# Splitting queries and keys on POOL, and a new order of fills, in a 16-head attention kernel

## The chip, the cores and the metric

The kernel runs on one core of a Trainium2 chip. The metric is the device time of one execution in microseconds, the median of several runs. The engines are called PE (TensorE, matmuls), DVE (VectorE), ACT (ScalarE), POOL (GpSimd) and SP (the queue that issues most transfers).

## The reference, cut to what matters

`x` is 32 batches of 128 rows of width 128, with a condition vector and a context of 128 rows for each batch. The first block, all in float32:

```python
x_norm = modulate(_ln(x), shift_a, scale_a)             # self attention, 16 heads of 8
q, k, v = split(x_norm @ W_qkv + b_qkv)
attn = softmax(q @ k.T * 8 ** -0.5) @ v
x = x + gate_a[:, None] * (attn @ W_proj + b_proj)
q_c = _ln(x) @ W_qc + b_qc                              # cross attention
k_c, v_c = split(_ln(context) @ W_kvc + b_kvc)
x = x + softmax(q_c @ k_c.T * 8 ** -0.5) @ v_c @ W_cproj + b_cproj
x = x + gate_m[:, None] * (gelu(modulate(_ln(x), shift_m, scale_m) @ W_mlp1 + b_mlp1) @ W_mlp2 + b_mlp2)
```

A second block attends to 128 learned keys and mixes three small experts by a router. The change touches nothing of it.

## The kernel before, in words

**Tiling.** The batches form 8 groups of 4. Self and cross attention of every group make 16 half loads, of which each iteration i = 0 to 7 of `attention_loop` holds two ("memories" 0 and 1, table `HOLDS`). An iteration treats 8 batches ("cores" in the code), each in 4 units of 4 heads, so it has 32 steps of one unit; there are 256 units in all. For each unit PE computes the scores (L1683), DVE takes their negated row maxima over the keys (L1518, into `NM`), later PE computes the scores a second time, transposed and with the maxima subtracted (the "shifted" scores, L1696), ACT takes the exponential (L1399) and PE multiplies with the values (L1712). Scores run `LEAD` = 14 steps ahead of the shifted ones. Iteration -1 is the lead-in: only loads, norms, fills and the first 14 score units. Iterations 5 and 6 are called crossed: both memories hold cross attention and the steps come from `crossed_steps`; iterations 1 to 4 use `regular_steps`, 0 and 7 own mixtures.

**How the maxima enter.** Two batches make a pair, four pairs an iteration. After the last reduction of a pair, DVE splits the maxima into two bf16 parts `M2`: `high` (L1529, a copy that casts) and `low` (L1531, the difference). PE turns them (`max_turn`, L1724), ACT copies them (L1413), and SP moves them as extra rows into the query stack. `max_parts` and `max_turn` stand at steps 2, 10, 18 and 26.

**Queries and keys in three parts.** For an f32-like product of bf16 operands, q and k are split into high, middle and low bf16 parts (`Qp`, `Kp`). PE fills a bank with `W x XT` (the "fill", L1763), ACT reads it and writes the high part as bf16 with the bias added (L1454), DVE computes `rest = bank + bias - high` in f32 (L1630), and POOL makes the middle part, `rest` + 0 cast to bf16 (L1352), and the low part, `rest` - middle (L1355). SP then moves each part to 8-row strides of the stacks `Qs` and `Ks`, 6 moves for each of q and k (L1280); the first K of all goes by ACT's queue. Three stacks are used in turn. Stack 0 of the next iteration is first read by the score of step 18, stack 1 by that of step 34 (2 of the next iteration). All fills but a few of the first ones share one bank, PS6, so each waits until the one before has been read.

**Order.** No planner: every engine walks the same list of events, `attention_events`, sorted by the written times (in steps) of `regular_steps`, `crossed_steps`, `first_steps` and `stack_steps`, and does its own part of each event in that order. A `fill_steps(t, name, n, (part, at))` is PE's fill at t and the reads at `at` (part 0 is ACT's, part 1 DVE's and POOL's for q and k). `stats_steps` are layer norm statistics on DVE (L1571, L1579), with the reciprocal deviation on POOL (L1321, L1324); `norm_steps` are two POOL operations (L1342, L1345). `load_steps` is SP's load of a context group, which waits until the norm of the one before is done. Names such as k0, q1, v1 are the memory's; xt_s, xt_x, xt_c are the turned norms of self, cross query and context; proj and yt the projection and its turn back.

Of the kernel before, what the change touches and what calls it, by code (L numbers as in the profile page):

```python
# [21 lines left out]
ALU = mybir.AluOpType  # L22
# [3 lines left out]
P = 128  # L26
# [123 lines left out]
def regular_steps(i):  # L150
# [9 lines left out]
            + fill_steps(12.0, "proj_c", i - 3, (1, 12.1))  # L160
            + fill_steps(14.0, "yt_c", i - 3, (1, 14.1))
            + fill_steps(16.0, "xt_c", i - 1, (1, 16.1))
# [3 lines left out]
            + fill_steps(26.0, "v0", i + 1, (1, 26.1))  # L166
            + fill_steps(28.0, "proj_s", i + 2, (0, 28.1), (1, 28.2))
            + fill_steps(30.0, "yt_s", i + 2, (1, 30.1)))


def crossed_steps(i):

    g = 2 * i - 6
    return (load_steps(0.1, g + 1) + stats_steps(4.2, 5.2, "ln_c", g + 1) + norm_steps(6.0, "ln_c", g + 1)
            + stats_steps(11.2, 12.2, "ln_x", g + 1) + norm_steps(14.0, "ln_x", g + 1)
            + load_steps(9.0, g + 2) + stats_steps(18.2, 19.2, "ln_c", g + 2) + norm_steps(20.0, "ln_c", g + 2)
            + fill_steps(1.0, "xt_c", g, (1, 1.1)) + fill_steps(3.0, "k0", i + 1, (0, 3.1), (1, 4.0))
            + fill_steps(6.0, "xt_x", g, (1, 6.1)) + fill_steps(8.0, "q0", i + 1, (0, 8.1), (1, 9.0))
            + fill_steps(11.0, "v1", i, (1, 11.1))
            + fill_steps(13.0, "proj_c", i - 3, (1, 13.1)) + fill_steps(15.0, "yt_c", i - 3, (1, 15.1))  # L180
            + fill_steps(17.0, "xt_c", g + 1, (1, 17.1)) + fill_steps(19.0, "k1", i + 1, (0, 19.1), (1, 20.0))
            + fill_steps(22.0, "xt_x", g + 1, (1, 22.1)) + fill_steps(24.0, "q1", i + 1, (0, 24.1), (1, 25.0))
            + fill_steps(27.0, "v0", i + 1, (1, 27.1)))


# [1679 lines left out]
```

## Time and profile before

| | us |
|---|---|
| median of 3 runs | 617.23 (615.05 to 619.32) |
| profiled execution | 618.34, span 616.6 |
| PE busy | 558.4 (91%) |
| DVE busy | 445.8 (72%) |
| ACT busy | 379.8 (62%) |
| POOL busy | 221.0 (36%) |
| mean granted clock of PE | 0.962 |

Busy time is the time in which an engine runs at least one instruction; PE's matmuls overlap, so a busy PE need not be at its peak. The granted clock is a share of TensorE's full speed, 2.4 GHz; 0.5 is its lower level, 1.2 GHz. An idle engine costs nothing by itself; only the chain of waits tells what sets the end.

### The profile page before, as it was taken

The numbers are of one execution on the slowest core, as the hardware profiler recorded it, in microseconds if no ns is written. First come the engines' busy times: TensorE is split into PE (matmuls) and PEld (weight loads), VectorE is DVE, ScalarE is ACT, GpSimd is POOL, SyncE is SP. The second block draws the span as 40 slices with busy tenths as digits, with TensorE's granted clock in tenths as the row PEclk, the third lists the DMA queues.
The fourth block names the chain that finished last, engine by engine and source line by source line (L and its number), as shares of the span: only waits on it lengthen the run. The fifth ranks groups of instructions, "written<-read, shape, count | busy, mean of one in ns | idle before, by whom it ended". The sixth has DMA issues, their size and how long they took to land.

```text
span 616.6 us, 16374 instructions
## 1 busy us (share of the span) xinstructions
PE 558.4 (91%) x6153; PEld 388.7 (63%) x6153; DVE 445.8 (72%) x1233; ACT 379.8 (62%) x889; POOL 221.0 (36%) x246
## 2 busy tenths in 40 slices
PE   3668999999999988898899989988999999999995
PEld 2354566666666655565567634445788788788785
DVE  7587999999999887978775635554475775775555
ACT  2236778787787875766776654563554754754762
POOL 6735635364654346435501310223123123123100
PEclk9768999999999997988999999998999999999999
DMA  7523645344343234233300010000000001000000
GB/s 206 128 81 94 177 142 147 84 125 108 98 117 94 75 107 122 71 83 85 106 3 5 2 35 0 1 0 18 16 10 28 26 11 34 23 11 19 17 18 18
DMA packets 48554, 39.24 MB, mean 64 GB/s; under 512 B 6209, under 2 KB 47842, under 8 KB 48482
## 3 DMA queue, kind: packets, MB, share of 16 engines
q1 hardware_dynamic: 46296, 34.49, 20.7%
q10 hardware_dynamic: 2186, 3.77, 2.1%
q8 instruction: 47, 0.77, 0.5%
q14 instruction: 25, 0.20, 0.1%
HBM read 9.93 MB, written 2.10 MB: 20 GB/s over the span
## 4 chain that ended last, share of the span: by engine, by line
PE 60%; DVE 22%; ACT 8%; issue 6%; DMA 2%; ACTq 1%; SPq 0%; POOL 0%; DVEq 0%; POOLq 0%
PE PS L910 30%; DVE NM L1518 7%; PE PS L1712 6%; PE PS L1683 5%; PE PS L1763 4%; PE PS L1775 3%; PE PS L947 3%; DVE rest L1630 2%; PE PS L1768 2%; PE PS L1734 2%; DVE M L1529 2%; PE PS L1696 1%; PE PS L1756 1%; PE PS L1779 1%; DVE M L1531 1%
## 5 line engine op out<-in xcount | busy, mean ns | idle before, releaser
L1518 DVE TENSOR_REDUCE NM<-PS 128x4 f32<-128x512 f32 x256 | 163.1, 682 | 20.1 <-PE PS L1683 19.8
L1399 ACT ACTIVATE PR<-PS 128x512 f32<-128x512 f32 x256 | 139.8, 600 | 31.8 <-PE PS L1696 31.7
L1683 PE MATMUL PS<-Ks,Qs 64*128 64x128 bf16 x1024 | 85.2, 224 | 6.3 <-DVE NM L1518 3.9
L713 ACT ACTIVATE r_HID<-PS,ANC 128x128 f32<-128x128 f32 x224 | 63.2, 370 | 43.8 <-PE PS L910 43.7
L1683 PEld LDWEIGHTS PS<-Ks,Qs 64*128 64x128 bf16 x1024 | 59.6, 97 | 47.6 <-issue 25.2
L1696 PE MATMUL PS<-Qs,Ks 64*128 64x128 bf16 x1024 | 85.9, 222 | 2.1 <-ACT PR L1399 1.4
L1712 PE MATMUL PS<-PR,Va 128*32 128x128 f32 x2048 | 84.3, 283 | 0.0
L1712 PEld LDWEIGHTS PS<-PR,Va 128*32 128x32 f32 x2048 | 49.6, 111 | 29.5 <-ACT PR L1399 18.5
L1696 PEld LDWEIGHTS PS<-Qs,Ks 64*128 64x128 bf16 x1024 | 58.2, 95 | 6.9 <-ACT PR L1399 4.8
L910 PE MATMUL PS<-r_NXS,r_WNS 128*128 128x512 f32 x168 | 54.2, 431 | 5.2 <-ACT r_HID L713 5.2
L631 POOL TENSOR_TENSOR m_veps<-m_mv,m_eps 128x4 f32<-128x4 f32 x16 | 3.2, 201 | 143.5 <-DVE m_mv L787 143.5
L910 PE MATMUL PS<-r_EVS,r_US 128*128 128x512 f32 x168 | 47.7, 392 | 0.0
L910 PE MATMUL PS<-WO,r_HID 128*128 128x128 f32 x384 | 45.5, 275 | 0.0
L910 PEld LDWEIGHTS PS<-WO,r_HID 128*128 128x128 f32 x384 | 44.7, 192 | 0.7 <-ACT r_HID L713 0.2
L1763 PE MATMUL PS<-XT,W 128*128 128x512 f32 x64 | 39.9, 712 | 4.4 <-ACT XT L1435 4.4
L910 PEld LDWEIGHTS PS<-r_NXS,r_WNS 128*128 128x128 f32 x168 | 28.6, 189 | 14.5 <-ACT r_HID L713 8.0
L910 PEld LDWEIGHTS PS<-r_EVS,r_US 128*128 128x128 f32 x168 | 31.5, 188 | 7.4
L910 PE MATMUL PS<-m_H,W 128*128 128x512 f32 x64 | 33.7, 628 | 1.5 <-DVE YT L810 1.5
L1352 POOL TENSOR_TENSOR Kp<-rest,zeros 128x512 bf16<-128x512 f32 x16 | 16.6, 1038 | 48.4 <-DVE rest L1630 48.4
L693 ACT ACTIVATE m_H<-PS,V 128x512 f32<-128x512 f32 x32 | 21.3, 693 | 19.7 <-PE PS L910 19.7
L910 PE MATMUL PS<-m_XT,W 128*128 128x512 f32 x64 | 32.1, 601 | 0.3 <-ACT m_XT L705 0.3
L1321 POOL TENSOR_TENSOR veps<-mv,eps 128x4 f32<-128x4 f32 x24 | 4.8, 202 | 72.3 <-DVE mv L1579 72.3
(183 smaller groups left out, 1074.6 us busy)
## 6 DMA issues: line engine op xcount, KB each, us to landing
Qs<-Qp SPq DMA_DIRECT2D x96, 128.0 KB
Ks<-Kp SPq DMA_DIRECT2D x90, 128.0 KB
CTXG<-in_ctx SPq DMA_DIRECT2D x8, 256.0 KB, 3.4
r_CTX<-in_ctx SPq DMA_DIRECT2D x8, 256.0 KB, 2.8
out<-X SPq DMA_DIRECT2D x8, 256.0 KB, 2.3
X<-in_x SPq DMA_DIRECT2D x7, 256.0 KB, 6.6
W<-in_weights ACTq DMA_DIRECT2D x2, 855.0 KB
Qs<-MT SPq DMA_DIRECT2D x62, 8.0 KB
```

The source lines that it names most:

```text
L693: nc.scalar.activation(H[:, k, :], FIRST_BANK[k % 2][:, :], ACT.Gelu_apprx_tanh, bias=vec("bmlp1", k))\
L713: last = nc.scalar.activation(HID[:, k, b * P:(b + 1) * P], HIDDEN_BANK[k % 2][:, b * P:(b + 1) * P], ACT.Silu, bias=ANC[:, k, bass.ds(g * ...
L910: return nc.tensor.matmul(to, lhsT, rhs, start=start, stop=stop)
L947: last = nc.tensor.transpose(bank[:, b * P:(b + 1) * P], source(b), ident[:, :])
L1352: nc.gpsimd.tensor_tensor(parts[:, 1, :], left, zeros[:, :].to_broadcast([P, GT]), ALU.add)\
L1399: nc.scalar.activation(PR[:, u, :], T_BANK[u % 2][:, :], ACT.Exp, scale=SCALE)\
L1518: nc.vector.tensor_reduce(out=NM[:, c.b // 2, c.second, u // 2, u % 2 * 4:u % 2 * 4 + 4], in_=S_BANK[score_bank(c, u)[0]][:, :].rearrange( ...
L1683: last = nc.tensor.matmul(S_BANK[bank][:, j * P:(j + 1) * P], Qs[c.stack][rows, lo + j, cols], Ks[c.stack][rows, lo + j, cols], start=True ...
L1696: last = nc.tensor.matmul(T_BANK[u % 2][:, j * P:(j + 1) * P], Ks[c.stack][rows, lo + j, cols], Qs[c.stack][rows, lo + j, cols], start=Tru ...
L1712: last = nc.tensor.matmul(O_BANK[p.turn][TW * j:TW * j + TW, at:at + P], Va[c.mem][:, c.b, 4 * (u // 2) + j, u % 2 * TW // 2:u % 2 * TW // ...
L1763: last = nc.tensor.matmul(PS[fill_bank(name, g)][:, :], w(WEIGHT[name[0]][kind]), source(name, g)[:, :], start=True, stop=True)
L1775: last = nc.tensor.matmul(GROUP_BANK[:, :], w(("proj", "cproj")[KIND[name]]), OgT[KIND[name]][:, :], start=True, stop=True)
```

## The change

1. Except for iteration 0 and for q0 and k0 of iteration 1 (`split_by_dve`), ACT now writes the f32 sum of bank and bias into `rest` and frees the bank; POOL makes the high part (`rest` + 0, cast), subtracts it from `rest` in place, and then makes middle and low as before. DVE has no part in it. ACT waits for the low part of the other memory before it overwrites `rest`.
2. The two operations that split the maxima are both written as scalar_tensor_tensor: `high = max(1.0 * nm, nm)` and `low = 1.0 * nm - high`.
3. Fills, statistics, norms and context loads have new times. In regular iterations fills after the first come 1 to 3 steps earlier, in crossed ones they start at 0.2 instead of 1.0; K and Q moves of memory 1 come 2 steps earlier; the second context load of a crossed iteration moves from 9.0 to 12.0, behind a norm at 7.0.
4. Lead-in: k1 and q1 of iteration 0 are filled and read before the first score, v1 at step 27; a dummy exponential of one column is done at step 5.6; behind each of the 14 score units PE runs a filler matmul of 512 columns into a bank that nobody reads.

```diff
-            + stats_steps(18.2, 19.2, "ln_c", i) + norm_steps(20.0, "ln_c", i)
-            + stats_steps(2.2, 3.2, "ln_x", i - 1) + norm_steps(7.0, "ln_x", i - 1)
+            + stats_steps(19.2, 20.2, "ln_c", i) + norm_steps(23.0, "ln_c", i)
+            + stats_steps(2.2, 3.2, "ln_x", i - 1) + norm_steps(9.5, "ln_x", i - 1)
             + fill_steps(0.2, "xt_s", i + 3, (0, 0.3), (1, 2.1))
             + fill_steps(4.0, "q0", i + 1, (0, 4.1), (1, 4.2))
-            + fill_steps(7.0, "k0", i + 1, (0, 7.1), (1, 8.0))
-            + fill_steps(10.0, "v1", i, (1, 10.1))
+            + fill_steps(6.0, "k0", i + 1, (0, 6.1), (1, 6.2))
+            + fill_steps(8.0, "v1", i, (1, 8.1))
...
-            + fill_steps(18.0, "k1", i + 1, (0, 18.1), (1, 19.0))
-            + fill_steps(21.0, "xt_x", i - 1, (1, 21.1))
-            + fill_steps(23.0, "q1", i + 1, (0, 23.1), (1, 24.0))
+            + fill_steps(16.0, "k1", i + 1, (0, 16.1), (1, 16.2))
+            + fill_steps(18.0, "xt_x", i - 1, (1, 18.1))
+            + fill_steps(20.0, "q1", i + 1, (0, 20.1), (1, 20.2))
...
 def crossed_steps(i):
-    return (load_steps(0.1, g + 1) + stats_steps(4.2, 5.2, "ln_c", g + 1) + norm_steps(6.0, "ln_c", g + 1)
-            + stats_steps(11.2, 12.2, "ln_x", g + 1) + norm_steps(14.0, "ln_x", g + 1)
-            + load_steps(9.0, g + 2) + stats_steps(18.2, 19.2, "ln_c", g + 2) + norm_steps(20.0, "ln_c", g + 2)
-            + fill_steps(1.0, "xt_c", g, (1, 1.1)) + fill_steps(3.0, "k0", i + 1, (0, 3.1), (1, 4.0))
-            + fill_steps(6.0, "xt_x", g, (1, 6.1)) + fill_steps(8.0, "q0", i + 1, (0, 8.1), (1, 9.0))
+    return (load_steps(1.0, g + 1) + stats_steps(5.2, 6.2, "ln_c", g + 1) + norm_steps(7.0, "ln_c", g + 1)
+            + stats_steps(13.2, 14.2, "ln_x", g + 1) + norm_steps(15.0, "ln_x", g + 1)
+            + load_steps(12.0, g + 2) + stats_steps(21.2, 22.2, "ln_c", g + 2) + norm_steps(23.0, "ln_c", g + 2)
+            + fill_steps(0.2, "xt_c", g, (1, 0.3)) + fill_steps(2.0, "k0", i + 1, (0, 2.1), (1, 2.2))
+            + fill_steps(4.0, "xt_x", g, (1, 4.1)) + fill_steps(6.0, "q0", i + 1, (0, 6.1), (1, 6.2))
...
 def first_steps():
-            + fill_steps(5.0, "k1", 0, (0, 18.7), (1, 18.8))
-            + fill_steps(19.6, "q1", 0, (0, 20.7), (1, 20.8))
-            + fill_steps(21.6, "v1", 0, (1, 22.7))
+            + fill_steps(5.0, "k1", 0, (0, 5.1), (1, 5.2))
+            + fill_steps(5.3, "q1", 0, (0, 5.4), (1, 5.5))
+            + fill_steps(27.0, "v1", 0, (1, 27.1))
+            + [(5.6, "init", "exp", 0, 0)]
...
+                if i == -1 and at >= 32 - LEAD:
+                    yield ("keep_busy", at)
...
+        def split_by_dve(name, it):
+            return it == 0 or it == 1 and name in ("q0", "k0")
...
+                    if not split_by_dve(name, it):
+                        mem = int(name[1])
+                        pool.wait_ge(stacked[stack_of(mem, it - 1)], stack_count(mem, it - 1))
+                        nc.gpsimd.tensor_tensor(parts[:, 0, :], left, nothing, ALU.add).then_inc(high_ready[name], 1)
+                        pool.wait_ge(high_ready[name], it + 1)
+                        nc.gpsimd.tensor_tensor(left, left, parts[:, 0, :], ALU.subtract).then_inc(left_ready, 1)
+                        pool.wait_ge(left_ready, 4 * (it - 1) + LEFT_ORDER[it].index(name) - 1)
...
+                    else:
+                        act.wait_ge(low_ready[name[0] + "10"[int(name[1])]], it + int(name[1]))
+                        nc.scalar.activation(rest[:, "qk".index(name[0]), :], GROUP_BANK[:, :], ACT.Identity, bias=bias)\
+                            .then_inc(bank_read[name], 1)
...
-                    nc.vector.tensor_copy(high, nm).then_inc(max_high, 1)
+                    nc.vector.scalar_tensor_tensor(high, nm, 1.0, nm, ALU.mult, ALU.max).then_inc(max_high, 1)
                     dve.wait_ge(max_high, c.n + 1)
-                    nc.vector.tensor_tensor(low, nm, high, ALU.subtract)\
+                    nc.vector.scalar_tensor_tensor(low, nm, 1.0, high, ALU.mult, ALU.subtract)\
                         .then_inc(max_parts, 1)
...
+                elif name == "keep_busy":
+                    nc.tensor.matmul(T_BANK[0][:, :], identb[:, :], Ks[0][:, 0, :], start=True, stop=True)
```

## Rows read from the trace of the kernel before

**Rows 1.** Busy us by window (start:end length, PE, PEld, DVE, ACT, POOL, clock, DMA, GB/s).

```profile
47.30:84.70 37.40, 33.60 (x571) 20.95 (x569) 32.68 (x84) 26.36 (x56) 18.56 (x20) 0.96 0.44 120
120.40:156.40 36.00, 35.02 (x593) 22.64 (x593) 33.75 (x88) 28.60 (x62) 18.63 (x20) 1.00 0.38 101
228.30:272.40 44.10, 39.44 (x597) 25.93 (x597) 35.74 (x96) 28.88 (x61) 21.88 (x24) 0.88 0.33 88
272.40:312.60 40.20, 36.13 (x594) 23.74 (x593) 32.27 (x74) 27.70 (x57) 19.39 (x20) 0.96 0.31 83
331.00:616.60 285.60, 265.34 (x1587) 197.66 (x1584) 164.80 (x531) 159.61 (x437) 60.35 (x68) 0.98 0.05 16
```

**Rows 2.** Chain that ended last, 157 to 183 us: start, us, engine, tile, line.

```profile
157.47 0.70 ACT Qp L1454
...
160.07 1.05 PE PS L1763 x2
...
162.63 0.57 PE PS L1712 x16
...
164.30 0.16 PE PS L1683
...
164.87 0.16 PE PS L1724 x2
...
167.16 0.59 PE PS L1734 x4
...
181.23 1.03 DVE M L1529
```

**Rows 3.** Groups by line, whole span: busy us, mean ns, idle before.

```profile
L1529 DVE CAST M<-NM 128x32 bf16<-128x32 f32 x32 | 13.7, 429 | 0.9
L1355 POOL TENSOR_TENSOR Kp<-rest,Kp 128x512 bf16<-128x512 f32 x16 | 18.7, 1170 | 1.3
L1324 POOL TENSOR_TENSOR rstd<-veps,half 128x4 f32<-128x4 f32 x24 | 24.4, 1018 | 1.9
```

**Rows 4.** Instructions of single lines: ns min/median/max, first and last start.

```profile
L1630 DVE SCALAR_TENSOR_TENSOR rest<-PS,V,Qp x16: 742/750/752, 20.8 to 301.7; 128x512 f32<-128x512 f32 x16
L1531 DVE TENSOR_TENSOR M<-NM,M x32: 191/192/1045, 38.6 to 331.0; 128x32 bf16<-128x32 f32 x32
```

**Rows 5.** Timeline of a crossed iteration, 236 to 239 us: start, us, engine, line.

```profile
237.10 0.71 DVE L1529 CAST M<-NM 128x32 bf16<-128x32 f32 x1
237.74 1.04 POOL L1352 TENSOR_TENSOR Qp<-rest,zeros 128x512 bf16<-128x512 f32 x1
237.85 0.97 DVE L1531 TENSOR_TENSOR M<-NM,M 128x32 bf16<-128x32 f32 x1
```

**Rows 6.** Waits, 228.3 to 312.6 us: total us, times, longest.

```profile
PE PS L1724 <- DVE M L1531: 7.1, 5, 2.1
```

**Rows 7.** Busy us of two stretches of low clock, columns as in rows 1.

```profile
36.90:50.50 13.60, 10.21 (x98) 6.37 (x102) 9.20 (x17) 6.39 (x14) 1.68 (x1) 0.50 0.03 9
238.20:245.10 6.90, 6.22 (x48) 4.51 (x48) 5.17 (x17) 1.95 (x4) 5.03 (x6) 0.51 0.54 148
```

**Rows 8.** SP's timeline near 170 us, and PE's DMA wait at 172.2 us.

```profile
167.92 2.91 SPq L1280 DMA_DIRECT2D Ks<-Kp  x3
...
PEld PS L1683 <- DMA Ks<-Kp: 0.8, 1, 0.8
```

**Rows 9.** Chain that ended last, lead-in.

```profile
24.16 3.86 DMA Qs<-Qp
...
32.13 1.74 PE PS L1768 x8
...
34.24 2.50 DVE NM L1518 x4
...
36.76 1.87 DVE M L1529
...
43.20 1.28 ACT L1399
```

More of the change, by code:

```diff
@@ L277 @@
 BANK_ORDER = list(dict.fromkeys(name for _, name, _ in FILLS if name != "mlp_xt"))
+LEFT_ORDER = [("q0", "k0", "k1", "q1") if HOLDS[0][it][0] == SELF else ("k0", "q0", "k1", "q1") for it in range(NG)]
 DERIVED = ("keys", "bias_out", "anchor", "u_low", "u_high", "wo_low", "wo_high")
@@ L301, in stack_steps @@
     steps += [(11 + 0.5 * k, 0, i + 1, *m) for k, m in enumerate(moves(second))]
-    return (steps + [(17.0, 1, i + 1, "zero", 0)] + [(21 + 0.5 * k, 1, i + 1, *m) for k, m in enumerate(moves("K"))]
-            + [(26 + 0.5 * k, 1, i + 1, *m) for k, m in enumerate(moves("Q"))])
+    return (steps + [(17.0, 1, i + 1, "zero", 0)] + [(19 + 0.5 * k, 1, i + 1, *m) for k, m in enumerate(moves("K"))]
+            + [(24 + 0.5 * k, 1, i + 1, *m) for k, m in enumerate(moves("Q"))])
 def stack_of(mem, it):
@@ L1280, in body @@
                     sp.dma_start(to, source).then_inc(stacked[k], 16)
-                elif name == "init":
+                elif name == "init" and ev[1] != "exp":
                     k = ("rest", "next", "third").index(ev[1])
@@ L1346, in body @@
                         .then_inc(ln_done[k], 1)
-                elif name == "read" and ev[1] in PARTS and ev[3] == 1                         and not (ev[1] == "q0" and at_first(ev[2])):
-                    name, g = ev[1:3]
+                elif name == "read" and ev[1] in PARTS and ev[3] == 1 and not (ev[1] == "q0" and at_first(ev[2])):
+                    name, it = ev[1:3]
                     parts, left = PARTS[name], rest[:, "qk".index(name[0]), :]
-                    pool.wait_ge(bank_read[name], g + 1)
-                    nc.gpsimd.tensor_tensor(parts[:, 1, :], left, zeros[:, :].to_broadcast([P, GT]), ALU.add)\
-                        .then_inc(middle_ready[name], 1)
-                    pool.wait_ge(middle_ready[name], g + 1)
+                    nothing = zeros[:, :].to_broadcast([P, GT])
+                    pool.wait_ge(bank_read[name], it + 1)
+                    if not split_by_dve(name, it):
[5 more added lines that the diff above has]
+                        pool.wait_ge(left_ready, 4 * (it - 1) + LEFT_ORDER[it].index(name) - 1)
+                    nc.gpsimd.tensor_tensor(parts[:, 1, :], left, nothing, ALU.add).then_inc(middle_ready[name], 1)
+                    pool.wait_ge(middle_ready[name], it + 1)
                     nc.gpsimd.tensor_tensor(parts[:, 2, :], left, parts[:, 1, :], ALU.subtract)\
@@ L1388, in body @@
                     act.dma_start(W[:, lo:hi], weights[:, lo:hi]).then_inc(load_w2, 16)
+                elif ev[:2] == ("init", "exp"):
+                    nc.scalar.activation(expt[:, :], bpr[:, 0:1], ACT.Exp, scale=0.0)
                 elif name == "stack" and of_scalar_queue(ev):
@@ L1620, in body @@
                         last.then_inc(bank_read[name], 1)
-                elif name == "read" and ev[1] in PARTS and ev[3] == 1:
+                elif name == "read" and ev[1] in PARTS and ev[3] == 1 and split_by_dve(*ev[1:3]):
                     name, it = ev[1:3]
-                    other, before = (name[0] + "1", it) if name[1] == "0" else (name[0] + "0", it + 1)
-                    if not isinstance(before, int) or before > 0:
-                        dve.wait_ge(low_ready[other], before)
+                    if it > 0 or name[1] == "1":
+                        dve.wait_ge(low_ready[name[0] + "10"[int(name[1])]], 1)
                     dve.wait_ge(high_ready[name], it + 1)
```

53 lines of the change are left out of this document (28 added, 25 removed).

## The prediction

> **What bounds the kernel now.** I read the busy time by iteration first [rows 1]. The windows run from the first query or key fill of an iteration to that of the next. A regular iteration (36.0 us, 32 steps, so 1.12 us a step; there are four between 84.7 and 228.3, 35.9 in the mean) has PE at 35.0 and DVE at 33.8 us, POOL at 18.6. The two crossed ones (i = 5 and 6) take 44.1 and 40.2 us for fewer fills, and their granted clock is 0.88 and 0.96 where the regular ones have 1.00. The first (47.3 to 84.7) takes 37.4. The 285.6 us after 331 are MLP and router, which the diff leaves alone.
>
> Then the chain inside one regular iteration [rows 2]. From 160 to 171 it is pure PE; from 171 to 183 it is DVE: reductions, two residuals (`rest`), and a `high` split of the maxima (CAST) of 1.03 us. So PE is the bound of one half and DVE of the other, and relief on DVE is worth only what PE leaves room for. The PE floor from these rows: the scores and shifted scores of two steps 0.57, their values 0.57, times 16 = 18.2; four q/k fills, two v and two projections, all taken at the q/k fill's 1.06 = 8.5; five turns of four blocks at 0.59 = 3.0; per pair a turn of 0.59, the turn back (taken as 0.37, between the 0.16 of two small turns and the 0.59 of four) and the maxima's 0.16, times 4 = 4.5. Sum 34.2 us, 1.7 below the 35.9 now.
>
> The durations [rows 3, 4]: `rest` on DVE 0.75 us x32; the split's CAST 429 ns in the mean, its TENSOR_TENSOR 192 in the median and 1045 at most. What lengthens these two is in the timeline of a crossed iteration [rows 5]: the CAST starts inside a POOL tensor_tensor and ends with it (0.71 us), the next POOL operation starts, and the TENSOR_TENSOR (0.97) ends with that. PE waits for it: 7.1 us in the two crossed iterations, up to 2.1 at once [rows 6]. Behind such a wait the granted clock is 0.51 for 6.9 us [rows 7]; this, not work, makes 44.1 out of 36. The second POOL operation is the copy of q's residual, released by the very `rest` that stands in front of the split on DVE, so the collision is systematic.
>
> **The change, part by part.**
>
> *Parts of queries and keys.* Six of 32 (iteration 0, and q0, k0 of 1) keep the old way. For 26, ACT writes f32 into `rest` instead of bf16 (same shape, 0.70 us, nothing); DVE loses 26 x 0.75 = 19.5 us, 3.0 an iteration. POOL gains a copy (1.04) and a subtraction with f32 output. The latter is not in the trace: between 1.04 (the copy, [rows 5]) and 1.17 (the subtraction to bf16, [rows 3]); I take 1.1. With gaps of 0.08 a part then takes POOL 4.6 us in four operations instead of 2.3, and POOL does 18.6 + 4 x 2.3 = 27.8 us of about 34.6, 80%. The group bank is free after ACT, not after DVE: 0.8 us earlier, of use only if the next fill waited. It does not.
>
> POOL becomes a clock of its own, so I walk its queue. Regular, from the iteration's start: q0 filled at step 4 and read at 6.2 us, parts 6.2 to 10.8, k0 to 15.4, cross norm (two of 1.04 with gaps, 2.2) to 17.6, statistics (0.2 + 1.02 with gaps, 1.3) and self norm to 21.1, k1 to 25.7, statistics 27.0, q1 31.6, context norm 33.8. Needed: stack 0 at step 18, 20 us. SP issues the last K move after the maxima's moves of step 10, as now; its landing already ended a PE wait once, by 0.8 us [rows 8]. A move takes 0.6 us and more to issue, and that one, issued by 170.8, had landed when PE went on at 173.0: 2.1, so k0's low part may come at 17.3 us, and comes at 15.4. Margin 1.9 us, 1.3 when steps shrink to 1.08. Stack 1 is needed at step 34, 37 us; q1's low part at 31.6 lands by 34.5. The next xt_c and xt_x have several microseconds.
>
> Crossed: k0 3.5 to 8.1, q0 8.3 to 12.9, statistics and context norm to 16.4, then cross norm to 19.9, k1 to 25.2, q1 to 29.8, statistics and norm to 33.3, where xt_c is filled at step 32.2, 34.5 us: margin 1 us. One step is late. The load of the second context group moved to step 12; it waits in SP's queue for that context norm (16.4), and the last two Q moves stand behind it. Three issues of 0.6, landing 2.1: 20.3 us, against 19.4 (18 steps of 1.08). Issues here average 0.97 in the row of three [rows 8], which makes it 21.4; I take 1.3 us of PE wait, between 0.9 and 2.0, in two iterations: +2.6. Bounds 0 and 6 (2 x 3, with the half clock behind it). The other displaced fills and statistics keep their number; what they displace has the margins above: +0.9.
>
> *The split's form.* Both operations become scalar_tensor_tensor. If POOL does not hold this form up, each costs 0.19 (the median of the TENSOR_TENSOR of the same shape [rows 4]). The trace has this form under POOL only as `rest`, 742 to 752 ns in all 16 of a form [rows 4], POOL at work or not, but there one operand is in PSUM; with both in SBUF it never starts under POOL. So cost from both sides: 0.19 (like `rest`, never held) or up to 1.0 more (like the TENSOR_TENSOR with two SBUF operands, 0.97). I take 0.19: the row of the same operation is the nearest. Per iteration DVE regains about 1.2 us in regular ones.
>
> The Trainium skill, "SBUF — State Buffer", section "SBUF: two separate sides", says a VectorE instruction with two SBUF inputs contends with a GpSimd one that reads SBUF, whatever the operation. The TENSOR_TENSOR's 0.97 us agrees; for the new form no row shows it. By that rule the result is the first rival's.
>
> *Sum for DVE and PE.* Regular and first iteration: DVE 33.8 - 3.0 - 1.2 = 29.6, no longer a bound; PE floor 34.2, and an in-order PE leaves some waits. I take 34.6: -1.3 x 5 = -6.5 (bounds 0 and -8.5).
> Crossed: of PE's 7.1 us of waits I take 5.5 back; clock 0.88 of 44.1 and 0.96 of 40.2 us make 13.8 us at half, of which 5.5 come back; DVE relief 1: -12 (bounds -4 and -15; then 36.2 each, above the floor of some 34.9).
>
> *Lead-in* [rows 9]. The chain waits 3.86 us for the last Q move; the q1 fill (at half clock twice the 1.05) behind it moves into this wait, and v1's 1.74 moves to step 27. Eight reductions of 0.63 (four in 2.50) from 29.5 then let the split start at 34.5 instead of 36.8: -2.3. The CAST of 1.87 us, which ended with a POOL memset, is 0.19: -1.7 (the memsets now follow q1 earlier, so they are over by then). The exponential's table load of 1.28 goes under the wait: -1.3. 14 filler matmuls of 512 bf16 columns go behind the scores; not in the trace, between 0.14 (as many columns in sixteen of 128, two groups at once, at 0.57) and 0.53 (half of an f32 fill). At 0.2 they fit into the 0.63 of a reduction, at half clock barely: +0.5. Half of 13.6 us at 0.50 [rows 7] lies after the first exponential; if the clock is up, -1.7. Sum -6.5 (bounds -3 and -9).
>
> **Total**: -6.5 - 6.5 - 12 + 2.6 + 0.9 = -21.5 against the profiled execution's 618.3 (span 616.6), giving 596.8. That execution is 1.1 above the median of 617.2; I keep 597.
>
> **Rivals.**
> - *The split is still held* (no row excludes it; for it stands the TENSOR_TENSOR). With POOL at 80% each of four splits an iteration waits 0.45 for the first (0.8 x half an operation) and as much for the second: 3.6 against 1.2 us now. DVE gains 0.6 net and PE waits at the maxima instead. Regular iterations unchanged, crossed ones lose only the systematic trigger (-5), lead-in -6, late moves +3.5, some half clock +2: about 613, 604 to 625.
> - *Slower: POOL misses stack 0.* Place: PE's first score of step 18. It decides if the low part of k0 (or q0) comes later than 17.3 us after the iteration's start. 1.3 us of margin is eaten by one extra statistics step or DVE's holding POOL once. Then PE waits some 1.5 us in each of seven iterations, and the half clock behind it (3.2 us, as in the window with 0.96) costs 1.6 more: 7 x 3.1 = 22, and the crossed iterations keep half of their present loss (+6): 625, up to 635. Against it: ready times are early in the queue, POOL idles until q0.
> - *DVE relief is worth nothing since PE bounds*: regular 0, the rest as forecast but the crossed at -7: 608.
>
> **Chances.** Forecast 0.57 (590 to 605), held split 0.22, late POOL 0.12, PE bound 0.09. About 1% (6 us) can be told from no change, so faster means below 611. Of the held split 0.09 lies below 611, 0.10 between, 0.03 above 623.4; late POOL gives 0.01 to the middle; PE bound 0.08 and 0.01. Faster 0.74, same 0.12, slower 0.14. The low bounds of all terms sum to -32.5, or 586. The range goes from 588, since they hardly fall together, to 616, leaving out the upper part of the held split and late POOL.
>
> **What would show it.** The split's two operations near 0.19 us, all 32; `rest` on DVE 6 times; regular iterations at 34.6 with POOL near 28; crossed ones at 36 with a clock of 1.00; no PE wait on the maxima above 0.5 us; PE waiting for a Q move at step 18 of the crossed ones; first exponential near 39 us. Wrong if the split shows 1 us under POOL, if PE waits for DMA in regular iterations, or if these stay at 35.9 with DVE idle.

## The result, and the profile after

The changed kernel takes 616.15 us in the median of 13 runs (606.68 to 621.14), the kernel before 617.23 of 13 (613.92 to 621.33): the medians of all runs differ by 1.1 us. The changed kernel's runs fall into two groups, six from 606.7 to 613.1 and seven from 616.2 to 621.1, and the mean granted clock goes with them (0.977 to 0.991 in the lower group, 0.958 to 0.969 in the upper). All ratios in this document are ratios of fast runs, those at most 1.5% above a kernel's fastest; here they are the lower six against all 13 of before, and the ratio is 0.988, interval 0.984 to 0.992. So the lower group is 7.5 us faster (1.2%), where the forecast said 20, and the upper one is no faster than before. The profiled execution took 616.67 us (span 614.8, clock 0.966) and so belongs to the upper group; a second profile of the same kernel (experiment 1) has a span of 605.7. Both are read here.

The attention part by iteration, in us, from the starts of every 32nd exponential (the windows of [rows 1] began with fills; these boundaries differ by a few us and sum to the span):

| kernel | first exponential | i=0 | 1 | 2 | 3 | 4 | 5 | 6 | 7 | rest |
|---|---|---|---|---|---|---|---|---|---|---|
| before | 44.5 | 37.6 | 35.7 | 36.0 | 35.9 | 35.6 | 44.7 | 40.6 | 37.0 | 269.0 |
| after | 47.3 | 38.2 | 37.0 | 36.4 | 36.5 | 35.0 | 39.0 | 36.6 | 41.1 | 267.7 |
| after, second profile | 40.0 | 38.3 | 37.1 | 36.4 | 36.4 | 35.1 | 39.0 | 36.6 | 37.0 | 269.8 |

The whole gain stands in iterations 5 and 6: 85.3 us became 75.6. The regular ones got longer: 143.2 us of iterations 1 to 4 became 144.9. The first exponential and iteration 7 differ between two executions of the same kernel by 7.3 and 4.1 us; less 2.1 us in the rest, that is all of the 9.1 us between them.

Busy time by window of the kernel after: start:end and length, then PE, PEld (loads of PE's weights), DVE, ACT, POOL, granted clock, DMA share, GB/s. Iterations 2, 3, 5, 6, 7 and the lead-in's stretch of low clock:

```profile
122.50:158.90 36.40, 34.38 (x600) 22.41 (x596) 31.56 (x84) 28.18 (x61) 27.25 (x28) 1.00 0.37 100
158.90:195.40 36.50, 34.30 (x604) 22.32 (x600) 31.86 (x84) 27.62 (x59) 27.24 (x28) 1.00 0.38 99
230.40:269.40 39.00, 35.34 (x608) 22.94 (x608) 34.76 (x93) 28.93 (x60) 31.95 (x34) 1.00 0.37 100
269.40:306.00 36.60, 34.13 (x594) 22.35 (x592) 30.95 (x70) 27.41 (x56) 29.83 (x30) 1.00 0.36 96
306.00:347.10 41.10, 39.46 (x537) 27.70 (x532) 25.18 (x65) 23.70 (x49) 6.50 (x8) 0.88 0.01 3
23.30:47.20 23.90, 22.64 (x102) 10.79 (x104) 13.31 (x31) 5.14 (x10) 11.08 (x10) 0.50 0.45 107
```

Beside [rows 1]: POOL rose from 18.6 to 27.25 us in a regular iteration (forecast 27.8), DVE fell from 33.8 to 31.6 where 29.6 was forecast, PE from 35.0 to 34.4, and the iteration did not get shorter. The crossed iterations have their clock back: 1.00 where [rows 1] have 0.88 and 0.96.

Most of DVE's other 2 us are in the two operations of the split. They are shown by line (ns as minimum, median and maximum), with the residual that DVE keeps and POOL's new subtraction:

```profile
L1555 DVE SCALAR_TENSOR_TENSOR M<-NM x32: 181/193/707, 37.2 to 327.0; 128x32 bf16<-128x32 f32 x32
L1557 DVE SCALAR_TENSOR_TENSOR M<-NM,M x32: 191/193/1166, 37.4 to 327.2; 128x32 bf16<-128x32 f32 x32
L1654 DVE SCALAR_TENSOR_TENSOR rest<-PS,V,Kp x3: 750/751/752, 18.2 to 54.3; 128x512 f32<-128x512 f32 x3
L1369 POOL TENSOR_TENSOR rest<-rest,Kp x13: 1155/1164/1218, 69.1 to 291.3; 128x512 f32<-128x512 f32 x13
```

The same by group, busy us and mean ns:

```profile
L1557 DVE SCALAR_TENSOR_TENSOR M<-NM,M 128x32 bf16<-128x32 f32 x32 | 15.6, 487 | 1.1
L1555 DVE SCALAR_TENSOR_TENSOR M<-NM 128x32 bf16<-128x32 f32 x32 | 8.6, 269 | 1.1
```

Together 24.2 us; before, the CAST took 13.7 [rows 3] and the TENSOR_TENSOR 10.1. In iterations 2 and 3 the eight operations of the split take 2.6 and 3.0 us, as before (2.7 and 2.6), where 1.5 was forecast: that is 1.3 of the 2 us. The rest is that DVE's operations overlap in the trace (in these iterations of before they last 39.5 us each in sum, in 33.8 of busy time), so one that is left out takes less off the busy time than its duration. The median is 193 ns, but 11 of the 32 second operations take 961 to 1166 ns. The timeline of iteration 3 shows one of them (start, us, engine, line; POOL and DVE only):

```profile
177.97 1.04 POOL L1356 TENSOR_TENSOR XN<-XN,rstd 128x512 f32<-128x512 f32 x1
...
178.38 0.68 DVE L1555 SCALAR_TENSOR_TENSOR M<-NM 128x32 bf16<-128x32 f32 x1
...
178.97 1.04 POOL L1367 TENSOR_TENSOR Kp<-rest,zeros 128x512 bf16<-128x512 f32 x1
179.10 0.96 DVE L1557 SCALAR_TENSOR_TENSOR M<-NM,M 128x32 bf16<-128x32 f32 x1
...
180.11 0.23 PE L1751 MATMUL PS<-identb,M 128*32 128x128 bf16 x2 [1.12 <-DVE M L1557]
```

Both operations start inside a POOL operation and end 50 ns behind its end (179.01 and 179.06; 180.01 and 180.06). It is the picture of [rows 5] with the new form in it, and PE idles 1.12 us for it. In the first crossed iteration:

```profile
242.09 0.19 DVE L1555 SCALAR_TENSOR_TENSOR M<-NM 128x32 bf16<-128x32 f32 x1
242.27 1.16 POOL L1373 TENSOR_TENSOR Qp<-rest,Qp 128x512 bf16<-128x512 f32 x1
242.31 1.17 DVE L1557 SCALAR_TENSOR_TENSOR M<-NM,M 128x32 bf16<-128x32 f32 x1
```

All four second operations of iteration 5, and three of the four of 6, are held like this. What PE waited for in the two crossed iterations (228 to 306 us: total, times, longest):

```profile
PE PS L1751 <- DVE M L1557: 3.8, 6, 1.1
...
PE PS L1707 <- DMA Qs<-Qp: 0.9, 1, 0.9
```

The 7.1 us of [rows 6] are 3.8, none longer than 1.1, and the forecast's late Q move is there with 0.9 us.

In the lead-in, the chain that ended last now runs through the fillers (L1712):

```profile
24.35 3.83 DMA Qs<-Qp
...
28.90 0.54 PE PS L1712
29.44 0.54 PE PS L1707 x4
...
38.62 0.54 PE PS L1712
```

A unit of scores and a filler take 1.08 us, where the reduction behind a unit takes 0.63 [rows 9]. PE, not DVE, sets the lead-in, and at half clock throughout.

In the regular iterations the waits of PE can be compared (total, times, longest). First for iterations 2 and 3 of before (117.8 to 189.7 us), then for the same two after (122.5 to 195.4 us):

```profile
PE PS L1724 <- DVE M L1531: 0.7, 2, 0.4
...
PE PS L1683 <- DVE NM L1518: 0.3, 2, 0.2
```

```profile
PE PS L1751 <- DVE M L1557: 1.9, 2, 1.1
PE PS L1707 <- DVE NM L1544: 1.1, 2, 0.6
```

Before, PE waited for DVE 1.3 us in the two iterations together (with 0.3 for a third line), so by these waits relief on DVE could give some 0.7 us an iteration. After, it waits 3.2 us (with 0.2 for a third): the change made PE wait more for DVE, not less.

### The profile page after: what moved, and what is told of

It is laid out like the page before. It is cut to its first block, busy times and chain, and to the rows that moved or that the text cites. A ratio compares the mean times of both kernels' runs of the same rounds, so it can differ in the third digit from the quotient of the medians.

```text
span 614.8 us, 16429 instructions
## 1 busy us (share of the span) xinstructions
PE 561.2 (91%) x6167; PEld 387.8 (63%) x6167; DVE 431.0 (70%) x1207; ACT 376.9 (61%) x890; POOL 277.4 (45%) x298
## 4 chain that ended last, share of the span: by engine, by line
PE 62%; DVE 15%; ACT 8%; issue 6%; DMA 5%; POOL 2%; SPq 1%; ACTq 1%; DVEq 0%; POOLq 0%
PE PS L915 28%; PE PS L1739 7%; PE PS L1707 6%; PE PS L1790 4%; DVE NM L1544 4%; PE PS L1802 2%; PE PS L952 2%; PE PS L1761 2%; PE PS L1795 2%; PE PS L1723 2%; DMA Qs<-MT 2%; PE PS L1783 2%; DVE M L1557 1%; DMA Qs<-Qp 1%; ACT PR L1420 1%
## 5 line engine op out<-in xcount | busy, mean ns | idle before, releaser
L1544 DVE TENSOR_REDUCE NM<-PS 128x4 f32<-128x512 f32 x256 | 163.7, 681 | 40.8 <-PE PS L1707 39.9
L1707 PEld LDWEIGHTS PS<-Ks,Qs 64*128 64x128 bf16 x1024 | 59.6, 97 | 58.5 <-issue 27.8
L1707 PE MATMUL PS<-Ks,Qs 64*128 64x128 bf16 x1024 | 86.6, 224 | 6.0 <-DVE NM L1544 3.8
L915 PE MATMUL PS<-WO,r_HID 128*128 128x128 f32 x384 | 45.5, 275 | 0.0
L915 PEld LDWEIGHTS PS<-WO,r_HID 128*128 128x128 f32 x384 | 44.7, 192 | 0.7
L1790 PE MATMUL PS<-XT,W 128*128 128x512 f32 x64 | 38.6, 694 | 5.6 <-ACT XT L1456 5.1
L890 DVE TENSOR_TENSOR r_T<-PS,BO 128x384 f32<-128x384 f32 x32 | 17.7, 552 | 17.8 <-PE PS L915 17.6
L1480 ACT ACTIVATE rest<-PS,V 128x512 f32<-128x512 f32 x26 | 17.9, 687 | 19.8 <-PE PS L1790 19.7
```

The lines of the kernel that those rows point to most:

```text
L890: nc.vector.tensor_tensor(t, EXPERT_BANK[b % 2][:, 0:NE * P], BO[:, 0:NE * P], ALU.add)\
L915: return nc.tensor.matmul(to, lhsT, rhs, start=start, stop=stop)
L1480: nc.scalar.activation(rest[:, "qk".index(name[0]), :], GROUP_BANK[:, :], ACT.Identity, bias=bias)\
L1544: nc.vector.tensor_reduce(out=NM[:, c.b // 2, c.second, u // 2, u % 2 * 4:u % 2 * 4 + 4], in_=S_BANK[score_bank(c, u)[0]][:, :].rearrange( ...
L1707: last = nc.tensor.matmul(S_BANK[bank][:, j * P:(j + 1) * P], Qs[c.stack][rows, lo + j, cols], Ks[c.stack][rows, lo + j, cols], start=True ...
L1790: last = nc.tensor.matmul(PS[fill_bank(name, g)][:, :], w(WEIGHT[name[0]][kind]), source(name, g)[:, :], start=True, stop=True)
```

## The experiments

The numbers of this section are medians, with the ratio to the kernel before on the same chip and its interval.

**1. The same kernel again.**

> The changed kernel as it is, for a second profile. Theory L (the clock in the lead-in and at the end of attention decides between two times): its runs fall near 609 or near 619, and the profile near 609 lacks the half clock of 10.2 us that the first profile had at 323.7 us, or has a shorter one than 23.9 us in the lead-in. Rival: the half clock stretches are the same and the difference comes from waits for transfers.

Measured: 613.5 us in the median of 4 (607.5 to 620.6); the profile has a span of 605.7. The chain of its lead-in:

```profile
28.86 0.32 PE PS L1712
29.18 0.33 PE PS L1707 x4
...
34.70 0.32 PE PS L1712
```

The windows of its low and its first full clock, columns as above:

```profile
24.60:28.00 3.40, 3.02 (x4) 0.67 (x2) 1.33 (x7) 1.03 (x2) 2.47 (x4) 0.50 0.98 181
28.00:40.00 12.00, 11.52 (x104) 6.63 (x104) 10.24 (x18) 3.36 (x7) 8.62 (x7) 1.00 0.51 136
```

The same instructions in the same order, at 1.00 here and at 0.50 above, 40.0 against 47.3 us. Iterations 0 to 6 agree within 0.2 us in the two profiles, so they can be compared from one profile each; the first exponential and iteration 7 can't.

**2. Without the fillers.** The two lines that emit `keep_busy` are taken out.

> The changed kernel without the 14 filler matmuls of the lead-in. Theory F (each filler costs 0.54 us at half clock, and one unit then takes 1.08 instead of the 0.63 of a reduction): first exponential near 42 us instead of 47.3, total 4 to 5 us shorter than the changed kernel. Rival: without fillers the clock stays at half for longer into iteration 0, which gives back 3 us or more, total within 2 us of the changed kernel.

Measured: 610.6 us (608.1 to 613.5), ratio to before 0.987 (0.981 to 0.992). The first exponential is at 40.4 although the clock is 0.5 for 17.1 us. In the six profiles here of kernels with the new lead-in, whole reductions and no fillers (experiments 2, 6, 9, 11, 12) it comes at 39.8 to 40.6; in those with fillers at 39.6, 40.0, 40.1, 45.5, 45.7, 47.2 and 47.3. So the reordering is worth 4 us at the first exponential (44.5 to 40.4) and 3 at the end of iteration 0 (82.1 to 79.0, as that iteration takes 38.6), and the fillers cost nothing or 5 to 7 us at the first exponential, as the clock falls.

**3. POOL with most times old.** `regular_steps`, `crossed_steps`, `early_statistics` and `round_steps` of before put into the kernel after. The stack moves of memory 1 kept their new places (19 and 24), and the lead-in stayed new; experiment 11 has the moves at their old places too.

```diff
-            + fill_steps(6.0, "k0", i + 1, (0, 6.1), (1, 6.2))
+            + fill_steps(7.0, "k0", i + 1, (0, 7.1), (1, 8.0))
...
-            + fill_steps(20.0, "q1", i + 1, (0, 20.1), (1, 20.2))
+            + fill_steps(23.0, "q1", i + 1, (0, 23.1), (1, 24.0))
```

> The changed kernel (parts on POOL, new form of the split, new lead-in) with the regular, crossed and stack times of the kernel before. Theory H (what the moved work gained went into waits behind POOL, whatever the order): regular iterations stay at 35.5 to 36.5 us and the total within 4 us of the changed kernel. Rival T (the new times are what spoils the regular iterations, or what saves them): with the old times they take 34.6 us, total 602 to 606; or the parts come too late for stack 0, PE waits for transfers and the total is above 625.

Measured: 618.9 us (10 runs), 1.002 (0.998 to 1.005). PE's DMA waits from 78 to 228 us:

```profile
PE PS L1707 <- DMA Ks<-Kp: 4.5, 4, 1.8
...
PE PS L1723 <- DMA Qs<-MT: 2.2, 2, 1.2
```

**4. The new times on the kernel before.** The same four functions the other way; stack moves old, here too.

> The kernel before with the new regular, crossed and stack times alone; residuals stay on DVE and the old forms of the split stay. Theory T (the new times break the crossed iterations' collision of q's copy with the split): crossed iterations 38 us with clock 1.00 instead of 44.6 and 40.6, total near 608. Rival H: the residual in front of the split still releases POOL at the wrong moment, crossed iterations stay above 40 us, total 615 or more.

Measured: 627.3 us, 1.014 (1.011 to 1.018). Iterations 0 to 4 take 43.0, 39.3, 40.5, 38.8 and 39.9 us, the crossed ones 38.6 and 36.8. The new times alone cost some 4 us in each regular iteration (2.9 to 4.5) and give the crossed ones 10 us in all. The expectation had the crossed iterations right and missed the cost in the others, and with it the total (608 expected).

**5. The old forms of the split** in the kernel after (a CAST and a TENSOR_TENSOR).

```diff
-                    nc.vector.scalar_tensor_tensor(high, nm, 1.0, nm, ALU.mult, ALU.max).then_inc(max_high, 1)
+                    nc.vector.tensor_copy(high, nm).then_inc(max_high, 1)
...
-                    nc.vector.scalar_tensor_tensor(low, nm, 1.0, high, ALU.mult, ALU.subtract)\
+                    nc.vector.tensor_tensor(low, nm, high, ALU.subtract)\
```

> The changed kernel with the old forms of the split (a copy that casts, a tensor_tensor). Theory P (POOL holds up both forms of the second operation alike): the difference operation shows up to 1.16 us as in the new form, and the regular and crossed iterations and the total stay within 1 us an iteration of the changed kernel (607 to 620). Rival (the new form is worth its place): the crossed iterations go to 41 us or more and the total up by 5 us or more.

Measured: 614.1 us (10 runs), 0.995 (0.991 to 0.9995). Iterations 1 to 6 are 36.9, 36.4, 36.4, 35.4, 39.1, 36.6, each within 0.4 us of the kernel after; the second operation sums to 15.7 us as a TENSOR_TENSOR and to 15.6 as the new form. No worth of the form shows.

**6. No split at all.** The reduction writes bf16 maxima straight into `M2`, the low part is zero and set once; both split operations are left out, so the maxima subtracted are rounded (in exact arithmetic a softmax does not depend on what is subtracted).

```diff
-                    nc.vector.tensor_reduce(out=NM[:, c.b // 2, c.second, u // 2, u % 2 * 4:u % 2 * 4 + 4],
+                    nc.vector.tensor_reduce(out=M2[:, c.b // 2, c.second, u // 2, 0, u % 2 * 4:u % 2 * 4 + 4],
...
-                    nc.vector.scalar_tensor_tensor(high, nm, 1.0, nm, ALU.mult, ALU.max).then_inc(max_high, 1)
...
-                    pe.wait_ge(max_parts, c.n + 1)
+                    pe.wait_ge(max_done, 8 * c.n + 8)
```

> The changed kernel in which the reductions write the maxima straight as bf16 into M2; the two split operations are gone, the low part is zero (the same rounded shift goes into all keys of a row, so the softmax is the same). Theory P (what the moved residuals gained is lost in the split's wait for POOL): regular iterations 36.4 to 35.0 us, crossed 39.0 and 36.6 to 36.5 and 35, total 10 us below the changed kernel. Rival B (PE's order of fills bounds the iterations, the wait is hidden): regular iterations stay within 0.5 us of 36.4.

> The same without the filler matmuls. Theory F (with the fillers the lead-in takes 40.0 us with a full clock or 47.3 at half, without them 40.4 at half): median 2 to 5 us below the direct maxima with fillers and less spread, 597 to 602 in all. Rival: equal medians, since the full clock in the lead-in is as frequent as not and worth more.

> The kernel before (residuals on DVE, old times, old lead-in) with the maxima written straight as bf16. Theory P (POOL holding the split is what made the crossed iterations slow and their clock fall): crossed iterations 44.7 and 40.6 to 37 us with no half clock, regular 35.9 to 35.2, total near 603. Rival B: crossed ones gain only the 2.1 us of the longest waits, total above 610.

Measured: on the kernel after 604.9 us, 0.975 (0.967 to 0.984); the same without fillers 601.2, 0.973 (0.968 to 0.978); on the kernel before 607.2, 0.982 (0.974 to 0.989). The split costs some 8 to 11 us in either kernel (0.975 over 0.988, 0.973 over 0.987, and 0.982). Iterations 2 to 6 of the second are 35.9, 35.3, 35.3, 36.5, 34.3.

On the kernel before, one expectation failed: without the split the crossed iterations were to fall to 37 us with no half clock. The second did (36.3 us), the first did not. Its window, and PE's longest wait in it:

```profile
219.60:262.80 43.20, 38.36 (x604) 24.68 (x604) 32.89 (x89) 29.03 (x61) 22.68 (x25) 0.92 0.34 90
```

```profile
PE PS L1677 <- DMA Qs<-Qp: 3.0, 1, 3.0
```

Here 3.0 us go to a Q move that comes late (PE goes on at 243.35), and the clock is at 0.50 from 242.2 for 6.8 us. In the kernel before nothing of this move shows, since PE stood for the split (2.1 us) and at half clock there. So the split's wait hid a second cause of the same size.

**7. The residuals on DVE, all else as after.** `split_by_dve` is always true, with the waits of before.

```diff
-            return it == 0 or it == 1 and name in ("q0", "k0")
+            return True
```

> The changed kernel with the residuals of all queries and keys back on DVE (ACT writes the high part, POOL makes two operations a part); new times, new lead-in, fillers and new form of the split stay. Theory M (the move to POOL is needed because the new times put all parts close together; it is worth 3 us an iteration against this kernel, which the old order did not need): regular iterations 39 to 40 us as with the new times alone, total near 622. Rival (the move is worth nothing, PE bounds): total within 3 us of the changed kernel.

Measured: 631.1 us (624.1 to 635.6), 1.025 (1.017 to 1.033). Iterations 1 to 4: 39.4, 40.6, 38.8, 40.0; crossed 39.1 and 36.8. It repeats experiment 4 with the stack moves' new times too. Waits of it from 120 to 235 us:

```profile
PEld PS L1709 <- DVE NM L1545: 19.7, 32, 1.2
...
DVE rest L1656 <- ACT Qp L1477: 8.1, 6, 2.5
...
ACT Qp L1477 <- PE PS L1792: 7.9, 6, 2.8
```

DVE, in order, stands at a residual until PE's fill and ACT's read are there, and the reductions behind it come late: the new times put DVE's part of k0, k1 and q1 0.2 step behind the fill, where the old ones left a step. That it is this, and not the fills' places, was not tried by itself.

**8. DVE with less work.** Experiment 6 without fillers, and each reduction reads half of the keys (64 of 128).

> Direct maxima, no fillers, and each reduction reads only the first half of the keys (the shift of a row is then the maximum over 64 keys; the softmax is the same as long as nothing overflows). DVE loses about 0.27 us in each of 256 reductions, 8.5 us an iteration. Theory B (PE's own work is the floor, 34.2 us by the sum of its pieces): regular iterations 34.2 to 34.6 us from 35.3 to 36.7, total 5 us lower. Rival D (DVE's place in each step, not its sum, holds PE): they fall below 34 us, total 590 or less.

Measured: 598.1 us, 0.968 (0.962 to 0.974). Its windows of iterations 1 to 4:

```profile
74.40:111.10 36.70, 34.64 (x602) 22.63 (x597) 21.19 (x77) 28.18 (x62) 27.25 (x28) 1.00 0.52 147
111.10:146.60 35.50, 34.35 (x600) 22.41 (x595) 21.04 (x77) 28.13 (x61) 27.22 (x28) 1.00 0.39 103
146.60:181.40 34.80, 34.00 (x600) 22.20 (x596) 21.08 (x77) 27.36 (x58) 27.21 (x28) 1.00 0.40 104
181.40:216.00 34.60, 33.97 (x596) 22.11 (x592) 20.94 (x77) 27.20 (x58) 24.78 (x26) 1.00 0.39 106
```

DVE is busy 21 of 35 us, 12.7 less than before, and the four iterations take 35.4 in the mean, against 35.8 in the kernel before and in experiment 6 without fillers. The mean hides two things. Iteration 1 is 1.0 us longer than before, and there PE waits for POOL's part of K:

```profile
PE PS L1699 <- DMA Ks<-Kp: 1.2, 1, 1.2
```

Iterations 2 to 4 take 35.5, 34.8 and 34.6, where before has 36.0, 35.9 and 35.6: 0.9 us less each in the mean, close to the 34.2 to 34.6 expected. This kernel also has the new times and POOL's added work; the same relief on the kernel before was not tried.

**9. Residuals on DVE or POOL, times old or new, without the split.** Experiment 6 without fillers, with most times old as in experiment 3, stack moves new (first), or with the residuals on DVE (second).

> Direct maxima, no fillers, parts on POOL, but the old regular, crossed and stack times. Theory T (with the wait for POOL gone, the new times only bring the parts forward in time for POOL's longer way to the stacks): first crossed iteration above 40 us and regular ones 36 to 37.5, total 5 to 10 us above the same kernel with new times (606 to 611). Rival: within 2 us of it, since the split's wait was all that the times answered to.

> Direct maxima, no fillers, new times, all residuals on DVE. Theory M: DVE again holds PE where the parts cluster, regular iterations 37 to 38 us, total 610 to 615, so the move to POOL is worth some 10 us once POOL no longer holds the split. Rival: 602 to 605, and moving the residuals was worth next to nothing even then.

Measured: 618.3 us, 0.999 (0.996 to 1.003), and 611.4, 0.991 (0.988 to 0.995). Regular iterations in the mean of 1 to 4: DVE with old times (experiment 6, third) 35.3, DVE with new 37.7, POOL with old 36.9, POOL with new 35.8. With the split the same four are 35.8, 39.7, 37.2 and 36.2 (POOL with all times old, experiment 11: 36.6, and 36.1 without the split). The two parts of the change belong together: each alone costs, and together they come back to within 0.5 us of where they began. The first of these two kernels was expected at 606 to 611; it is above, with 4.3 us of waits for `Qs<-Qp` and 2.2 for `Qs<-MT` in its crossed iterations.

**10. Only the crossed times.** The kernel before, with `crossed_steps`, `early_statistics` and the branches of iterations 5 and 6 new, and the stack moves of memory 1 new there.

```diff
+    if i >= NG - 3:
+        return (steps + [(17.0, 1, i + 1, "zero", 0)] + [(19 + 0.5 * k, 1, i + 1, *m) for k, m in enumerate(moves("K"))]
+                + [(24 + 0.5 * k, 1, i + 1, *m) for k, m in enumerate(moves("Q"))])
```

> The kernel before with nothing of the change but the times of the two iterations that feed crossed stacks (i = 5 and 6: fills, statistics, loads, and the stack moves of member 1 two steps earlier). Theory 'the gain lies in the crossed times alone': in earlier runs residuals on VectorE with all new times had crossed iterations of 38.6 and 36.8 us against 44.7 and 40.6 before, while its regular ones rose from 35.8 to 39.6; with the regular times left old, the regular ones stay at 35.8 and the crossed ones fall, -9 to -10 us: 607 us, better than the whole change (611 to 616). Rival 'the crossed iterations gain only because the regular ones left their work early': the crossed iterations stay above 41 us each on average and the time at 615 to 617.

Measured: 610.5 us, 0.989 (0.985 to 0.992): as much as the whole change. Windows of its crossed iterations, and PE's longest waits in them:

```profile
226.80:264.70 37.90, 35.45 (x601) 22.65 (x604) 34.25 (x95) 28.63 (x61) 21.96 (x25) 1.00 0.37 99
264.70:301.40 36.70, 34.67 (x592) 22.28 (x592) 31.94 (x75) 27.26 (x57) 21.12 (x22) 1.00 0.36 95
```

```profile
PE PS L1727 <- DVE M L1534: 1.3, 3, 0.5
...
PE PS L1686 <- DMA Qs<-Qp: 0.8, 1, 0.8
```

Here PE waits 1.3 us for the split, against 3.8 with POOL's added work. The two crossed iterations take 37.9 and 36.7 us, 10.7 less than before; iteration 4, in front of them, takes 37.0 instead of 35.6.

**11. Experiments 3 and 9 with all times old,** the stack moves' too (the lead-in stays new; the expectation on record names it wrongly among the old times). First with split and fillers, then without both.

> The changed kernel with the times of before for fills, statistics, lead-in and stack moves alike (the earlier run with old times had left the stack moves at their new, earlier places in the SP queue, steps 19 and 24). Theory 'the stall of TensorE for Qs<-MT in that run came from moves queued before their data': with the moves at 21 and 26 the waits for Qs<-MT go, regular iterations fall from 37.2 to 36.0 to 36.4, crossed ones stay above 38, 611 to 615 us. Rival 'POOL's parts come too late for the old times': Ks<-Kp waits of 5 us stay, 617 to 621 us.

> Maxima written in bf16 by the reductions (the low part of a maximum is zero and its two operations are left out), no filling matmuls, all three parts on POOL, and every time as before, the stack moves' too. Earlier with the moves two steps earlier: 618 against 601 with all new times. Theory 'early moves in the queue made it': 605 to 609 us. Rival 'POOL's lateness made it': 615 to 619 us.

Measured: 614.8 us (12 runs), 0.995 (0.991 to 0.999), and 608.9, 0.986 (0.981 to 0.990). The first one's iterations 1 to 6: 36.8, 36.6, 36.5, 36.4, 39.9, 36.9. Its DMA waits from 78 to 228 us:

```profile
PE PS L1707 <- DMA Ks<-Kp: 4.0, 4, 1.5
...
PE PS L1707 <- DMA Qs<-Qp: 1.2, 2, 0.7
```

The waits for `Qs<-MT` are gone from PE's list in these iterations (1.4 us stay in the crossed ones): they came from moves queued in SP ahead of their data, in front of the maxima's. Those for `Ks<-Kp`, 1 us in each iteration, stay: with the old fills POOL's parts come too late. Both theories held, for one wait each. And POOL alone also mends the crossed iterations (76.8 us against 85.3), so the change does this twice over. Without the split (second kernel) they take 41.7 and 36.7: there PE waits 3.5 us for `Qs<-Qp`, a move that was late all along and shows once the split is gone.

**12. Each part where it pays.** No split, no fillers, the new lead-in; residuals on DVE at old times up to iteration 5's parts, all three parts on POOL with new times for those of iterations 6 and 7.

```diff
-            return it == 0 or it == 1 and name in ("q0", "k0")
+            return it < NG - 2
```

> Maxima written in bf16 by the reductions (low part zero, split left out), no filling matmuls, the new lead-in, residuals on VectorE at the old times for the regular iterations, and all three parts on POOL with the new times only for the two crossed ones. Summing the best rows seen so far: first exponential 40.5, regular iterations 35.3 (as with direct maxima on the kernel before), crossed 36.5 and 34.3, last 37 to 41, tail 268 to 270: 593 to 599 us, against 601 for new times throughout. Rival 'TensorE's own busy time holds both': 600 to 602 us.

Measured: 598.7 us (597.6 to 602.3), 0.970 (0.967 to 0.973), 2.5 us under new times throughout (601.2, experiment 6), which is within what the two ranges leave open, and the fastest here of those whose reductions read all keys. The best rows summed to 593 to 599. Iterations 1, 2 and 5 to 7:

```profile
76.30:111.50 35.20, 34.74 (x604) 22.58 (x596) 31.39 (x80) 28.61 (x62) 18.52 (x20) 1.00 0.54 153
111.50:146.90 35.40, 34.79 (x602) 22.48 (x594) 31.26 (x80) 28.60 (x62) 18.53 (x20) 1.00 0.39 103
...
218.60:255.70 37.10, 34.62 (x604) 22.57 (x601) 29.00 (x83) 28.57 (x60) 30.63 (x33) 1.00 0.38 100
255.70:290.10 34.40, 33.64 (x594) 22.09 (x592) 26.46 (x63) 27.22 (x57) 29.75 (x30) 1.00 0.38 102
290.10:331.10 41.00, 39.36 (x536) 27.63 (x532) 24.15 (x59) 23.65 (x48) 6.50 (x8) 0.88 0.02 4
```

Iteration 1 has 35.2 us with DVE at 31.4 and POOL at 18.5, and experiment 8 has 35.4 in the mean with DVE at 21. PE itself is busy for 34.7 and 34.8 us of iterations 1 and 2 here, so PE bounds them. In iterations 3 and 4 (35.3 and 36.4) experiment 8 is 0.5 and 1.8 us shorter, so there it is not PE's work alone.

## Why the prediction was wrong

The size was wrong: 7.5 us came by the ratio (1.1 by the medians of all runs), 20 were forecast. The direction was right only at the edge: 0.988 of 617.23 is 609.7, and the prediction drew its line for faster at 611. By its terms, in us of the profiles against before; where two values stand, the first profile is first:

| term | forecast | measured | what settles it |
|---|---|---|---|
| lead-in | -6.5 | +2.8 or -4.5 | experiments 1, 2 |
| regular and first iteration | -6.5 | +2.3 or +2.5 | 5 to 9 |
| crossed, with the late moves | -9.4 | -9.7 | 6, 10, 11 |
| other | +0.9 | in the rows above | |
| iteration 7 and the rest | 0 | +2.8 or +0.8 | not settled |

- **The form of the split: wrong, and the first rival right.** The step that failed is "I take 0.19: the row of the same operation is the nearest". `rest` was the same operation but read one operand from PSUM; the TENSOR_TENSOR was another with the same two SBUF operands, and that was the nearer row: 961 to 1166 ns in 11 of 32. The Trainium skill's rule ("SBUF — State Buffer", section "SBUF: two separate sides"), by which two SBUF inputs against a GpSimd operation that reads SBUF decide, whatever the operation, agrees with these rows, though not with the small 128x4 operation on POOL that reads SBUF too and under which the second operation takes its 193 ns. DVE got 2.2 us back in a regular iteration, not 4.2, 1.3 of the difference by this. The wait that the change was to end is worth 8 to 11 us (experiment 6), and it did not end it.
- **Regular iterations: the floor was nearly right, the room above it was not.** The PE floor was put at 34.2 us; experiment 8 shows 34.2 busy in the mean, and its iterations 3 and 4 reach the 34.6 to 34.8 that were forecast, but only with 12.7 us of DVE work gone. The chain of before [rows 2] showed DVE for 12 us, and I read that as room for PE. PE's own waits show the room: 0.7 us an iteration for DVE before, half of the 1.3 that I took, and 1.6 after. The rival "PE bounds" (608) was nearer to this stage than the forecast.
- **New times were costed at nothing in the regular iterations.** With the residuals on DVE they cost 4 us each (experiments 4, 7), with POOL they save 0.4 over the old (36.2 against 36.6 in experiment 11). So POOL pays for what the times took, and for little more. That POOL would be late was priced as a rival at stack 0 with new times; in the kernel after PE waits for `Ks<-Kp` once, 1.0 us, but with old fills it does so every iteration. The walk through POOL's queue (parts of 4.6 us, 27.8 busy) held.
- **Crossed iterations: the sum right, by another way.** I had the half clock go because the split would no longer be held. Its second operation is held in 7 of 8 cases (4 of 8 before), but the waits are at most 1.1 us and the clock stayed at 1.00. "This, not work, makes 44.1 out of 36" was wrong as well: without the split the first crossed iteration of before still takes 43.2 us, for a late Q move (experiment 6). The new times mend both (36.5 us for that iteration without the split, experiment 6), so it is in part luck that the sum came out. The systematic trigger (POOL's copy released by the very `rest` in front of the split) is gone, and the new times keep it away without POOL as well. The late Q move cost 0.9 us, inside the bounds of 0 and 6; I took it for new with the change, and it was there before.
- **Lead-in: the reordering about right, the filler with the wrong size.** The three gains of the reordering (2.3, 1.7 and 1.3) were summed to 5.3 us; together they give 4 (experiment 2), with the split at 33.9 us where 34.5 was forecast. The filler was taken at 0.2 us each and at half clock as barely covered, +0.5 in all; it takes 0.32 at full clock and 0.54 at half, on a PE that then has 1.08 us for each 0.63 of DVE. It gives back the 4 us and 3 more, when the clock is low. The higher clock, for which 1.7 us were taken, came in one profile of the two.

What stays open: the relief of experiment 8 on the kernel before, with its own times, was not tried. Iteration 7 takes 41 us with 10.2 us of half clock in it, or 37 without, in executions of the same kernel (after: 41.1 and 37.0). It comes in kernels with and without the change's parts, so it isn't put down to them, and what lets the clock fall there was not tried.

## What to carry to other kernels

When an operation is held by another engine, change where its operands live or do away with it, and take as its price the row with the same operands, not that of the same opcode. Before work is moved off an engine that shares the chain, add up the waits of the bounding engine for it (0.7 us an iteration here, in the profile of before), and take most of its work away in an experiment: experiment 8 gives 0.4 us in the mean, for over a third of DVE's work. Parts of a change that are tuned to each other (who computes, and when) must be tried alone as well: here a third part, the times of two iterations, gave as much as the whole change. A wait that shows can hide another behind it: the split's 2.1 us hid a late move of 3.0.

## What was not expected of the hardware

- A VectorE scalar_tensor_tensor whose two tensor inputs are one and the same SBUF tensor (L1555) is held by POOL as well, up to 707 ns against 193.
- A held operation ends 47 to 50 ns behind the POOL operation (the CAST 36 to 39), less than its own 193 ns.
- Who starts first keeps the other waiting, and a tie goes to DVE: in all cases with POOL's start 41 ns or more ahead of a `low` operation and time left in a large POOL operation, DVE is held; where POOL starts within 7 ns of it, before or after (6 times after the change, 9 before it), DVE takes its 193 ns and POOL's subtraction is the longer one, 1214 to 1218 ns in the rows of L1369 against 1155. Under the small 128x4 operation that takes POOL 1.02 us, the new form is not held (193 ns). This is read from the timelines alone; no experiment moved the starts.
- The granted clock stayed at 0.50 for 23.9 us of one execution (PE busy 22.6 of them, and without a gap from 28.4 to 39.2) and for 3.4 us of another with the same instructions. Work put in to keep PE busy then ran at the lower clock and was itself the delay.
